# A vision tower on one core: weight splits at bursts 25 and 31 of an attention batch in place of 0 and 30, and a second buffer of raw weights in the sequence experts

## The chip, the core and the metric

The kernel runs on one core of a Trainium2 chip. The core has five engines that run side by side, each with its own list of instructions in order: TensorE (PE, matmuls and transposes), VectorE (DVE), ScalarE (ACT), GpSimd (POOL) and SyncE (SP). SP and POOL also issue DMA transfers. The engines meet at semaphores: an instruction can wait until a counter has reached a number, and everything behind it on its engine waits with it. The metric is the device time of one execution in microseconds (us); lower is better.

## The reference, cut to what matters

Two layers over x of 8 images with 1024 tokens each, 128 wide, in float32. Each layer is an attention and a mixture of 8 experts of which 2 are used (per image in the first layer, per token in the second).

```python
h = _L0_tok_ref(x, L0_tok_W)                       # embedding + position table
h = h + _L0_attn_ref(_layernorm(h), Wq, ..., gamma, beta)   # 8 heads, 1024 x 1024 scores per head pair
h = h + _L0_ffn_ref(_layernorm(h), ..., w1, b1, w2, b2)     # 2 of 8 experts per image
h = h + _L1_attn_ref(_layernorm(h), ...)                    # block attention
h = h + _L1_ffn_ref(_layernorm(h), Wr, W1, b1, W2, b2)      # 2 of 8 experts per token
```

The weights of all 16 experts (w1, w2 of the first layer, W1, W2 of the second: 32 matrices of 64 Ki floats) are used in matmuls as a sum of two parts, a high part rounded to the matmul's float32r format and a low part with the rest. The kernel makes these parts itself, one matrix (a "job") at a time, and stores them in HBM, from where the two expert stages load them.

## The kernel before

**Stages.** One after the other: a start (embedding of image 0), the first attention over 8 batches (one image each) with the embedding of the next image between its bursts, the sequence experts (first mixture), the block attention, the token experts (second mixture), and the sum of the results.

**Attention.** A batch is 32 bursts of two units. A unit is a pair of score matmuls on PE (L874) into PSUM, one exponential on ACT (L787) and four matmuls with the values (L886). PE, ACT and DVE each walk through the bursts in the same written order. The table STEPS (L549) puts the next image's work between them: "E" at bursts 1 and 3 (PE L802 embeds half an image into the PSUM bank psA; DVE L958 reads it, adds the position table and takes moments), "T" at 5 and 13 (PE L808 transposes), "q", "k", "N", and "v" at 27 and 29 (PE L823, read by DVE L976). All of these use the one bank psA: a step's matmuls wait until DVE has read the step before it (semaphore psA_free). At the start of each quarter (bursts 0, 8, 16, 24) DVE also adds a projected context (add_input, L460) and divides (L1069 to L1075); at the end of each quarter (7, 15, 23, 31) it takes the output out of PSUM (out_of_psum, L1065). At burst 28 POOL multiplies and adds tiles of the residual (L473 to L477).

**A weight job.** POOL loads a raw matrix into the tile raw (load_raw, L223), DVE splits it into the tile split (split_weights: a copy that rounds, L229, and a subtraction, L231), POOL stores split to HBM (store_split, L236) and at once issues the load of the next job, which may overwrite raw since the split is done. DVE's split waits until the job's raw matrix has landed (raw_in) and until the store of the job before has landed (split_out). There is one raw tile and one split tile. In attention the table SPLIT (L553) says at which bursts of a batch DVE and POOL do their part of a job: 2 jobs per batch, 16 in all, at the end of the burst's other work. Job 0 is loaded by POOL after it has cleared a tile for batch 1 (L760, L763).

**Sequence experts.** 32 items (image, half, expert); per item PE does 24 matmuls, ACT eight Gelu passes and an output (L1215), DVE four subtractions (L1295), each of which frees a tile that ACT writes again, and a weighted add (L1487). The class Rest places the other 16 jobs, one per item, at items 13 to 28, between the third and the fourth subtraction. SP loads the chosen experts' weights (1 MB each, L1434).

Of the kernel before, what the change touches and what calls it, by code (L numbers as in the profile page):

```python
# [8 lines left out]
F32 = mybir.dt.float32  # L9
F32R = mybir.dt.float32r  # L10
# [3 lines left out]
ALU = mybir.AluOpType  # L14
# [3 lines left out]
P = 128  # L18
EPS = 1e-5
CH = 512  # L20
# [5 lines left out]
class Tally:  # L26


    def __init__(self, start, parity=0):
        self.start, self.count, self.parity = start, 0, parity  # L30
# [128 lines left out]
class Shared:  # L159
# [8 lines left out]
    def __init__(self, nc, ctx, B, S, D, E):  # L168
        c = Core(nc, ctx, "ag")
        T, K = S // P, 2  # L170
        self.nc, self.B, self.T, self.K, self.E, self.D = nc, B, T, K, E, D
        self.JOBS = [(stage, e, layer) for stage in range(2) for e in range(E) for layer in range(2)]
        self.FIRST_JOBS = 2 * E
        self.raw, self.split = c.sb("raw", [P, CH]), c.sb("split", [P, 2, CH], F32R)
        self.raw_in, self.split_done = c.sem("raw_in"), c.sem("split_done")
        self.aw_sum = c.sb("aw_sum", [P, 1])
        self.n0 = [c.sb(f"n0{p}", [P, T, D]) for p in range(2)]
        self.res = [c.sb(f"res{p}", [P, TPC, D]) for p in range(2)]
        self.pe_tab = c.sb("pe_tab", [P, T, D])
        self.qs0, self.ks0 = (c.sb(n, [P, T, T // 2 * P], F32R) for n in ("qs0", "ks0"))  # L180
        self.w_in0 = [c.sem(f"w_in0{r}") for r in range(K)]
        self.f, self.f_done = self.n0[0][:, TPC:2 * TPC, :], c.sem("f_done")
        self.brow = c.sb("brow", [P, 5, D])
        self.w_raw = c.sb("w_raw", [D, 4, D])
        self.o_n, self.ctxT = c.sb("o_n", [P, CH]), c.sb("ctxT", [D, 2, P])
        self.stat_f, self.mv_f = c.sb("stat_f", [P, TPC, 6]), c.sb("mv_f", [P, TPC, 2])
        self.veps_f, self.rs_f = c.sb("veps_f", [P, TPC]), c.sb("rs_f", [P, TPC])
        self.dctx = [nc.dram_tensor(f"contexts{i}", [D, 2, P], F32).ap() for i in range(2)]
        self.norm_done, self.ctx_out, self.ctx_in, self.op_done, self.split_out, self.bias_in = (c.sem(n) for n in (
            "norm_done ctx_out ctx_in op_done split_out bias_in".split()))  # L190
        self.var_f, self.root_f, self.normal_done, self.stream_done = (c.sem(n) for n in "var_f root_f normal_done stream_done".split())

        self.attn_b, self.ones = c.sb("attn_b", [P, 1]), c.sb("ones", [P, P])
        self.gate_w, self.gate_b = c.sb("gate_w", [D, E]), c.sb("gate_b", [B, E])
        self.lower, self.places = c.sb("lower", [B, E, E]), c.sb("places", [B, 2, K, E])
        self.sc, self.e_sc = c.sb("sc", [P, B, T]), c.sb("e_sc", [P, B, T])
        self.zs, self.rz, self.corr = (c.sb(n, [P, B]) for n in ("zs", "rz", "corr"))
        self.mx, self.mxT, self.mx_row, self.mx_all = (c.sb(n, [P, 32]) for n in ("mx", "mxT", "mx_row", "mx_all"))
        self.mx4, self.mx1 = c.sb("mx4", [32, 4]), c.sb("mx1", [32, 1])
        self.base = c.sb("base", [P, 2 * T])  # L200
        self.pooledT = c.sb("pooledT", [D, B])
        self.lg, self.pr, self.rk = (c.sb(n, [B, 1, E]) for n in ("lg", "pr", "rk"))
        self.beats, self.ties = c.sb("beats", [B, 1, E, E]), c.sb("ties", [B, 1, E, E])
        self.nmx, self.sm, self.rsm = c.sb("nmx", [B, 1]), c.sb("sm", [B, 1]), c.sb("rsm", [B, 1])
        self.sel, self.val = c.sb("sel", [B, K, E]), c.sb("val", [B, K, E])
        self.g2, self.i2, self.i2i = c.sb("g2", [B, K]), c.sb("i2", [B, K]), c.sb("i2i", [B, K], I32)
        self.d_gate = nc.dram_tensor("d_gate", [B, K], F32).ap()
        self.d_chosen = nc.dram_tensor("d_chosen", [B, K], I32).ap()
        (self.tab_in, self.shift_done, self.exp_done, self.sum_done, self.gate_ps, self.pool_done,
         self.pooled_done, self.top_done, self.two_done, self.gate_out, self.gate_in) = (c.sem(n) for n in (  # L210
            "tab_in shift_done exp_done sum_done gate_ps pool_done "
            "pooled_done top_done two_done gate_out gate_in").split())

    def size(self, i):
        return self.GROUPS[i][1] - self.GROUPS[i][0]

    def load_raw(self, pool, j, ins):
        stage, e, layer = self.JOBS[j]
        src = ins[("w1", "W1")[stage]][e] if layer == 0 else ins[("w2", "W2")[stage]][e].rearrange("(n p) d -> p n d", p=P)
        dst = self.raw[:, :] if layer == 0 else self.raw[:, :].rearrange("p (n d) -> p n d", d=self.D)  # L220
        if j:
            pool.wait_ge(self.split_done, j)
        pool.dma_start(dst, src).then_inc(self.raw_in, 16)  # L223

    def split_weights(self, dve, j):
        dve.wait_ge(self.raw_in, (j + 1) * 16)
        if j:
            dve.wait_ge(self.split_out, j * 16)
        self.nc.vector.tensor_copy(self.split[:, 0, :], self.raw[:, :])  # L229
        dve.drain()  # L230
        self.nc.vector.tensor_tensor(self.split[:, 1, :], self.raw[:, :], self.split[:, 0, :].bitcast(F32), ALU.subtract).then_inc(self.split_done, 1)  # L231

    def store_split(self, pool, j, experts):
        stage, e, layer = self.JOBS[j]
# [285 lines left out]
def embed_and_attend(nc, H, ident, half, mean1, rstd1, score1, experts, shared, gate, chosen, ins, B, S, D, NH):  # L520
# [29 lines left out]
             20: ("N", 0), 21: ("N", 1), 27: ("v", 0), 29: ("v", 1)}  # L550
    FIRST = [("E", 0), ("E", 1), ("T", 0), ("q", 0), ("k", 0), ("T", 1), ("q", 1), ("k", 1), ("N", 0), ("N", 1), ("v", 0), ("v", 1)]
    LATE = 2
    SPLIT = [{0: 0, 30: 1}] * (B - 1) + [{5: 0, 12: 1}]  # L553
    GATES = {1: "biased", 3: "shift", 7: "sums", 9: "weights", 22: "pooled", 24: "ranks", 25: "choice", 30: "rows"}
    POOLED = {10: (0, 0), 11: (0, 1), 13: (0, 2), 14: (0, 3), 17: (1, 0), 18: (1, 1), 19: (1, 2), 20: (1, 3)}
    PE_TILES = {17: (4, 0), 18: (4, 1), 19: (5, 0), 20: (5, 1)}
    E, HID = ins["w1"].shape[0], ins["w1"].shape[2]
    assert shared.FIRST_JOBS == sum(map(len, SPLIT)) and HID == CH
    RESCUE = 25
# [7 lines left out]
    with ExitStack() as ctx:  # L567
        c = Core(nc, ctx, "a0")
# [152 lines left out]
        def _(pool):  # L721
# [20 lines left out]
            def batch(b, par, prior, more):  # L742
                for m in range(BURSTS):
# [8 lines left out]
                    if more and m == RESCUE - 1:  # L752
                        send_guard(pool, b + 1, 1 - par)
                    if m in SPLIT[b]:
                        j = b * len(SPLIT[b]) + SPLIT[b][m]
                        shared.store_split(pool, j, experts)
# [186 lines left out]
        def _(dve):  # L943
# [155 lines left out]
            def batch(b, par, prior, more):  # L1099
                for m in range(BURSTS):  # L1100
# [23 lines left out]
                    if more and m == RESCUE - 1:  # L1124
                        guard(b + 1)
                    if m in SPLIT[b]:
                        shared.split_weights(dve, b * len(SPLIT[b]) + SPLIT[b][m])

# [278 lines left out]
def sequence_experts(nc, H, ident, half, mean1, rstd1, score1, gate, chosen, shared, experts, ins, B, S, D):  # L1407

    parts = experts[0]
    E, _, WIDE = parts.shape  # L1410
    NB = (WIDE - 1) // (4 * P)
    T = S // P
# [5 lines left out]
    with ExitStack() as ctx:  # L1418
        c = Core(nc, ctx, "f0")
        f, f_done = shared.f, shared.f_done  # L1420
        w = [[shared.first_slot(r, WIDE) for r in range(K)], [c.sb(f"w1{r}", [P, WIDE]) for r in range(K)]]
        x_ps, t_ps, t_read, y_done, freed = (c.sem(n) for n in "x_ps t_ps t_read y_done freed".split())
        w_in = [shared.w_in0, [c.sem(f"w_in1{r}") for r in range(K)]]
# [3 lines left out]
        @block.sync  # L1427
        def _(sp):
            def load_parts(b):
                for r in range(K):  # L1430
                    e = sp.value_load(chosen[0:1, b * K + r:b * K + r + 1], min_val=0, max_val=E - 1)
                    if b >= 2:
                        sp.wait_ge(y_done, (b - 2) * PER + (PER - K + r + 1))
                    sp.dma_start(w[b % 2][r][:, :], parts[bass.ds(e, 1), :, :].rearrange("o p c -> p (o c)")).then_inc(w_in[b % 2][r], 16)  # L1434

            shared.load_sums(sp, B * T // 2 - 1)
            for b in range(1, 5):
                load_parts(b)
            shared.spread_gates(sp, 1, gate, chosen)
            load_parts(5)  # L1440
            sp.wait_ge(shared.gate_in, 64)
            for b in range(6, B):
                load_parts(b)

        @block.gpsimd
        def _(pool):
            b = B - 1
            shared.root_finish(pool, b, 0, 1, half)
            shared.root_finish(pool, b, 1, 0, half)
            shared.root_finish(pool, b, 1, 1, half)  # L1450
            shared.token_power(pool, 1)
            shared.gate_power(pool, 1)
            for j in range(shared.FIRST_JOBS, len(shared.JOBS)):
                shared.store_split(pool, j, experts)
                if j + 1 < len(shared.JOBS):
                    shared.load_raw(pool, j + 1, ins)
            pool.wait_ge(shared.split_out, 4 * E * 16)
            pool.wait_ge(shared.bias_in, 32)

# [752 lines left out]
```

## Time and profile before

| what | value |
|---|---|
| time, median of 3 runs | 1415.1 us (1413.77 to 1416.4) |
| the profiled execution: its own time | 1412.59 us |
| the profiled execution: span of its instructions | 1410.8 us |
| PE busy | 1184.4 us, 84% |
| ACT busy | 992.8 us, 70% |
| DVE busy | 917.3 us, 65% |
| POOL busy | 556.0 us, 39% |
| mean granted clock of TensorE | 0.916 of full speed |

Busy shares are means over stages with different limits. A wait in the views is idle time of an engine just before an instruction, with what ended it; it costs time only where the engine, or whoever waits for it, is the bound of its stage. Times in the views are us from the start of the span, so the profiled execution's own time is 1.8 us longer than what they cover.

### The profile page before, as it was taken

How to read it: one execution, taken by the hardware profiler on the slowest of the kernel's cores; microseconds unless marked ns; L12 is line 12 of the kernel's file. 1: busy time of each engine (PE TensorE's matmuls, PEld its weight loads, DVE VectorE, ACT ScalarE, POOL GpSimd, SP SyncE). 2: the span in 40 equal slices, each digit the busy share in tenths (PEclk: the TensorE clock that was granted, in tenths of full speed). 3: DMA queues.
4: the chain of work that ended last, by engine and by line, in shares of the span. 5: the costliest groups of instructions: out<-in, count | busy, mean ns of one | idle time of the engine just before them, and what ended most of it. 6: DMA issues, size and time to landing. Idle time of an engine off the chain costs nothing. (4 is left out here: it accounts for less than half of the span.)

```text
span 1410.8 us, 26930 instructions
## 1 busy us (share of the span) xinstructions
PE 1184.4 (84%) x9386; PEld 795.3 (56%) x9386; DVE 917.3 (65%) x2573; ACT 992.8 (70%) x1348; POOL 556.0 (39%) x538
## 2 busy tenths in 40 slices
PE   3499999999999999979898966888861799999940
PEld 2245444444444444558777755777761688888830
DVE  4255767777877776678687766888641466666625
ACT  0389889898989899869787855444410799999930
POOL 3413333333233332121011111478776177777660
PEclk9899999999999999989999987798955899999975
DMA  3645554554637282132226510011116377777609
GB/s 87 118 110 127 117 129 107 127 131 102 152 80 169 64 170 64 39 128 92 88 85 232 178 50 1 18 41 47 45 48 237 119 238 240 234 251 238 239 25 357
DMA packets 93162, 180.56 MB, mean 128 GB/s; under 512 B 15597, under 2 KB 64200, under 8 KB 84960
## 3 DMA queue, kind: packets, MB, share of 16 engines
q1 hardware_dynamic: 72832, 129.18, 33.1%
q0 software_dynamic: 17344, 42.68, 9.1%
q10 hardware_dynamic: 2848, 6.95, 1.7%
q8 instruction: 76, 1.25, 0.4%
q14 instruction: 62, 0.51, 0.1%
HBM read 116.96 MB, written 63.12 MB: 128 GB/s over the span
## 5 line engine op out<-in xcount | busy, mean ns | idle before, releaser
L787 ACT ACTIVATE a_probs<-a_psS 128x1024 f32<-128x1024 f32 x512 | 482.4, 1035 | 69.0 <-PE a_psS L874 57.5
L886 PE MATMUL a_psO<-a_probs,a_v 128*32 128x256 f32 x4096 | 277.4, 388 | 1.1 <-issue 0.7
L1295 DVE TENSOR_TENSOR f_g_lo<-f_g,f_g_hi 128x512 fp32r<-128x512 f32 x284 | 193.5, 688 | 117.7 <-ACT f_g L1202 116.5
L2039 POOL DMA_INDIRECT result<-f_out,f_idx x156 | 181.2, 1162 | 98.4 <-issue 58.5
L886 PEld LDWEIGHTS a_psO<-a_probs,a_v 128*32 128x32 f32 x4096 | 107.5, 109 | 133.9 <-issue 85.4
L1595 POOL DMA_INDIRECT queue<-all_row,all_idx x128 | 125.2, 978 | 38.0 <-issue 37.4
L1199 ACT ACTIVATE f_g_hi<-f_psH,all_w 128x512 fp32r<-128x512 f32 x156 | 109.3, 701 | 19.8 <-PE f_psH L72 18.6
L1202 ACT ACTIVATE f_g<-f_psH,all_w 128x512 f32<-128x512 f32 x156 | 109.2, 700 | 0.0
L874 PE MATMUL a_psS<-ag_qs,ag_ks 50*128 50x512 f32 x512 | 96.7, 454 | 9.6 <-DMA ag_qs<-a_gparts 7.1
L874 PE MATMUL a_psS<-a_qs,a_ks 50*128 50x512 f32 x512 | 95.1, 447 | 4.0 <-ACT a_probs L787 1.5
L465 POOL TENSOR_TENSOR ag_rs_f<-ag_veps_f,all_half 128x4 f32<-128x4 f32 x32 | 33.3, 1042 | 133.6 <-DVE ag_veps_f L135 133.6
L874 PEld LDWEIGHTS a_psS<-ag_qs,ag_ks 50*128 50x128 f32 x512 | 39.7, 190 | 57.0 <-ACT a_probs L787 30.3
L236 POOL DMA_DIRECT2D experts<-ag_split x32 | 18.2, 568 | 132.4 <-DVE ag_split L231 132.4
L1209 ACT ACTIVATE f_x_hi<-f_psX 128x512 fp32r<-128x512 f32 x55 | 33.1, 601 | 52.6 <-PE f_psX L1234 43.6
L70 PE MATMUL f_psH<-f_x_hi,all_w 128*128 128x512 f32 x156 | 68.6, 440 | 0.0
L874 PEld LDWEIGHTS a_psS<-a_qs,a_ks 50*128 50x128 f32 x512 | 38.8, 186 | 50.5 <-ACT a_probs L787 36.7
L71 PE MATMUL f_psH<-f_x_lo,all_w 128*128 128x512 f32 x156 | 62.2, 399 | 0.0
L72 PE MATMUL f_psH<-f_x_hi,all_w 128*128 128x512 f32 x156 | 62.0, 398 | 0.0
L70 PE MATMUL f_psY<-f_g_hi,all_w 128*128 128x512 f32 x156 | 61.6, 395 | 0.0
L72 PE MATMUL f_psY<-f_g_hi,all_w 128*128 128x512 f32 x156 | 61.4, 394 | 0.0
L71 PE MATMUL f_psY<-f_g_lo,all_w 128*128 128x512 f32 x156 | 61.4, 393 | 0.0
L1199 ACT ACTIVATE f_g_hi<-f_psH,f_w 128x512 fp32r<-128x512 f32 x64 | 44.6, 697 | 19.2 <-PE f_psH L72 18.7
(370 smaller groups left out, 2619.7 us busy)
## 6 DMA issues: line engine op xcount, KB each, us to landing
all_w<-experts SPq DMA_DIRECT2D x39, 1026.5 KB, 5.4
experts<-ag_split POOLq DMA_DIRECT2D x32, 512.0 KB, 4.2
f_rows<-queue SPq DMA_DIRECT2D x39, 260.0 KB
f_w<-experts SPq DMA_DIRECT2D x8, 1026.5 KB, 5.9
qparts<-a_parts SPq DMA_DIRECT2D x16, 512.0 KB, 3.6
kparts<-a_parts SPq DMA_DIRECT2D x14, 512.0 KB, 3.1
ag_qs<-experts SPq DMA_DIRECT2D x4, 1026.5 KB, 5.2
ag_ks<-experts SPq DMA_DIRECT2D x4, 1026.5 KB, 5.0
```

Source lines behind the costliest of these rows:

```text
L70: nc.tensor.matmul(out, w_lo, x_hi, start=first, stop=False)
L71: nc.tensor.matmul(out, w_hi, x_lo, start=False, stop=False)
L72: return nc.tensor.matmul(out, w_hi, x_hi, start=False, stop=last)
L465: self.nc.gpsimd.tensor_tensor(self.rs_f[:, :], self.veps_f[:, :], half[:, 0:TPC], ALU.pow).then_inc(self.root_f, 1)
L787: nc.scalar.activation(probs[u % NPR][:, :], psS[score_buffer(u)][:, :, :].rearrange("p a n -> p (a n)"), ACT.Exp).then_inc(exp_done, 1)
L874: last = nc.tensor.matmul(psS[score_buffer(u)][:, p, :], ks[par][64 * p:64 * p + KG, kt, hp * P:(hp + 1) * P], queries(par, hp, p, a), sta ...
L886: last = nc.tensor.matmul(psO[32 * g:32 * g + 32, a * HALF:(a + 1) * HALF], v[par][:, 2 * hp + p, kt, :], probs[u % NPR][:, cols:cols + HA ...
L1199: nc.scalar.activation(g_hi[i][:, n, :], psH[n][:, :], ACT.Gelu, bias=bias(m, n))
L1202: nc.scalar.activation(g[:, n, :], psH[n][:, :], ACT.Gelu, bias=bias(m, n)).then_inc(g_done, 1)
L1295: nc.vector.tensor_tensor(g_lo[i][:, n, :], g[:, n, :], g_hi[i][:, n, :].bitcast(F32), ALU.subtract).then_inc(lo_done, 1)
L1595: pool.indirect_dma_start(queue, bass.IndirectOffsetOnAxis(ap=idx[n % NROW][:, k, t:t + 1], axis=0), row[n % NROW][:, k, t, :], None).then ...
L2039: pool.indirect_dma_start(result, bass.IndirectOffsetOnAxis(ap=idx[i][:, j:j + 1], axis=0), out[i][:, j, :], None, bounds_check=2 * B * S ...
```

## The change

In batches 0 to 6 the two jobs move from bursts 0 and 30 to bursts 25 and 31; in batch 7 they stay. In the sequence experts a second raw tile (raw1) is added: its jobs use the two tiles in turn, job 17 is loaded by POOL at the start of the stage, and after the store of job j POOL loads job j + 2 in place of j + 1. There is still one split tile. Each raw tile has a semaphore of its own.

```diff
-        self.raw, self.split = c.sb("raw", [P, CH]), c.sb("split", [P, 2, CH], F32R)
-        self.raw_in, self.split_done = c.sem("raw_in"), c.sem("split_done")
+        self.raw, self.split = [c.sb("raw0", [P, CH])], c.sb("split", [P, 2, CH], F32R)
+        self.raw_in, self.split_done = [c.sem(f"raw_in{p}") for p in range(2)], c.sem("split_done")
...
+    def raw_place(self, j):
+
+        if j < self.FIRST_JOBS:
+            return 0, j + 1
+        r, i = divmod(j - self.FIRST_JOBS, 2)
+        return i, r + 1 + (0 if i else self.FIRST_JOBS)
+
+    def raw_freed(self, j):
+
+        return j if j <= self.FIRST_JOBS else j - 1
+
     def load_raw(self, pool, j, ins):
...
         if j:
-            pool.wait_ge(self.split_done, j)
-        pool.dma_start(dst, src).then_inc(self.raw_in, 16)
+            pool.wait_ge(self.split_done, self.raw_freed(j))
+        pool.dma_start(dst, src).then_inc(self.raw_in[i], 16)
 
     def split_weights(self, dve, j):
-        dve.wait_ge(self.raw_in, (j + 1) * 16)
+        i, loads = self.raw_place(j)
+        raw = self.raw[i]
+        dve.wait_ge(self.raw_in[i], loads * 16)
         if j:
             dve.wait_ge(self.split_out, j * 16)
...
-    SPLIT = [{0: 0, 30: 1}] * (B - 1) + [{5: 0, 12: 1}]
+    SPLIT = [{25: 0, 31: 1}] * (B - 1) + [{5: 0, 12: 1}]
...
+        shared.raw.append(c.sb("raw1", [P, CH]))
...
         @block.gpsimd
         def _(pool):
+            shared.load_raw(pool, shared.FIRST_JOBS + 1, ins)
...
             for j in range(shared.FIRST_JOBS, len(shared.JOBS)):
                 shared.store_split(pool, j, experts)
-                if j + 1 < len(shared.JOBS):
-                    shared.load_raw(pool, j + 1, ins)
+                if j + 2 < len(shared.JOBS):
+                    shared.load_raw(pool, j + 2, ins)
```

The order on DVE from burst 29 of a batch to burst 1 of the next, in the kernel before (a_v is the value tile, ag_split the split tile, a_o_t and ag_o_n the output of a quarter, all_H the residual):

```order
L976 TENSOR_TENSOR a_v<-a_psA,ag_brow 128x32x16
L229 CAST ag_split<-ag_raw 128x512
L231 TENSOR_TENSOR ag_split<-ag_raw,ag_split 128x512
L1065 STREAM_TRANSPOSE a_o_t<-a_psO 128x512
L460 TENSOR_TENSOR ag_res<-a_psA,ag_n 128x256
L1069 RECIPROCAL a_rden<-a_o_t 128x16
L1071 TENSOR_TENSOR a_o_t<-a_o_t,a_rden 128x16x16
L1075 STREAM_TRANSPOSE ag_o_n<-a_o_t 128x512
L229 CAST ag_split<-ag_raw 128x512
L231 TENSOR_TENSOR ag_split<-ag_raw,ag_split 128x512
L958 TENSOR_TENSOR all_H<-a_psA,ag_pe_tab 128x512
```

The same place on DVE in the changed kernel, whose lines stand 15 further down (L244 and L246 are the split, L1080 is out_of_psum, L973 is E's read):

```order
L991 TENSOR_TENSOR a_v<-a_psA,ag_brow 128x32x16
L1080 STREAM_TRANSPOSE a_o_t<-a_psO 128x512
L244 CAST ag_split<-ag_raw 128x512
L246 TENSOR_TENSOR ag_split<-ag_raw,ag_split 128x512
L475 TENSOR_TENSOR ag_res<-a_psA,ag_n 128x256
L1084 RECIPROCAL a_rden<-a_o_t 128x16
L1086 TENSOR_TENSOR a_o_t<-a_o_t,a_rden 128x16x16
L1090 STREAM_TRANSPOSE ag_o_n<-a_o_t 128x512
L973 TENSOR_TENSOR all_H<-a_psA,ag_pe_tab 128x512
```

No split stands between the division and E's read any more; one split has moved from ahead of out_of_psum to behind it.

DVE at bursts 25 to 29 of a batch in the changed kernel (L528 to L532 end burst 25's other work, L513 begins add_bias of burst 26, L991 is v's read):

```order
L532 SCALAR_TENSOR_TENSOR all_score<-all_score,ag_rs_f 128x4
L244 CAST ag_split<-ag_raw 128x512
L246 TENSOR_TENSOR ag_split<-ag_raw,ag_split 128x512
L513 TENSOR_TENSOR ag_res<-ag_res,ag_brow 128x512
L130 BN_STATS ag_stat_f<-ag_res 128x6 x4
L133 BN_AGGR ag_mv_f<-ag_stat_f 128x2 x4
L135 TENSOR_SCALAR ag_veps_f<-ag_mv_f 128x4
L991 TENSOR_TENSOR a_v<-a_psA,ag_brow 128x32x16
```

The two rows of the split are new here; the others are those of before, in their old order.

POOL at the start of the sequence experts in the changed kernel (L480 a root, L286 and L292 the gates' powers, L251 the store, L236 the load; f_raw is the second raw tile):

```order
L236 DMA f_raw<-W 128x4x128
L480 TENSOR_TENSOR ag_rs_f<-ag_veps_f,all_half 128x4 x3
L286 TENSOR_TENSOR ag_e_sc<-ag_base,ag_sc 128x16
L292 TENSOR_TENSOR ag_pr<-ag_base,ag_lg 2x8
L251 DMA experts<-ag_split 128x1024
L236 DMA ag_raw<-W 128x512
L251 DMA experts<-ag_split 128x1024
L236 DMA f_raw<-W 128x4x128
```

The first row is new. The load that stands behind a store is now that of the job after the next, into the tile that the split just done has read.

## Rows read from the trace of the kernel before

**Rows 1.** Windows: stretch, length, busy us of each engine (instructions), PEclk, DMA share, GB/s.
```profile
55.00:600.00 545.00, 527.06 (x5657) 254.33 (x5658) 377.63 (x1075) 481.69 (x514) 172.19 (x179) 0.99 0.48 110
600.00:845.00 245.00, 214.01 (x1010) 169.56 (x1003) 182.17 (x423) 184.18 (x306) 34.58 (x44) 0.95 0.36 123
```

**Rows 2.** Waits of the whole span: total us, times, longest us.
```profile
ACT a_probs L787 <- PE a_psS L874: 57.5, 74, 6.7
...
PE a_psA L808 <- DVE all_H L958: 5.5, 6, 1.5
...
DVE ag_split L229 <- DMA ag_raw<-w: 31.9, 7, 21.5
...
DVE ag_split L229 <- DMA ag_raw<-W: 20.6, 12, 3.4
```

**Rows 3.** Timeline, bursts 1 to 5 of batch 0: start, us, what [idle before].
```profile
62.04 1.15 PE L802 MATMUL a_psA<-a_w_tok,a_xt 29*128 29x128 f32 x8
...
69.31 0.43 DVE L229 CAST ag_split<-ag_raw 128x512 fp32r<-128x512 f32 x1 [21.45 <-DMA ag_raw<-w]
...
70.59 0.69 DVE L958 TENSOR_TENSOR all_H<-a_psA,ag_pe_tab 128x512 f32<-128x512 f32 x1
70.79 0.57 POOL L236 DMA_DIRECT2D experts<-ag_split  x1 [5.46 <-DVE ag_split L231]
...
71.33 2.07 PE L802 MATMUL a_psA<-a_w_tok,a_xt 29*128 29x128 f32 x8 [4.81 <-DVE all_H L958]
...
78.58 0.66 PE L808 MATMUL a_psA<-all_ident,ag_n 128*128 128x128 f32 x4
```

**Rows 4.** Timeline, bursts 1 to 5 of batch 1.
```profile
135.30 1.15 PE L802 MATMUL a_psA<-a_w_tok,a_xt 29*128 29x128 f32 x8
...
138.51 0.69 DVE L958 TENSOR_TENSOR all_H<-a_psA,ag_pe_tab 128x512 f32<-128x512 f32 x1
...
145.69 0.66 PE L808 MATMUL a_psA<-all_ident,ag_n 128*128 128x128 f32 x4 [1.50 <-DVE all_H L958]
```

**Rows 5.** Timeline, burst 27 of batch 2 to burst 1 of batch 3.
```profile
259.75 0.69 DVE L976 TENSOR_TENSOR a_v<-a_psA,ag_brow 128x512 f32<-128x512 f32 x1
...
262.48 1.16 PE L823 MATMUL a_psA<-ag_w_raw,a_nT 128*128 128x128 f32 x8
...
265.41 1.62 DVE L231 TENSOR_TENSOR ag_split<-ag_raw,ag_split 128x512 fp32r<-128x512 f32 x1
...
267.02 0.72 DVE L1065 STREAM_TRANSPOSE a_o_t<-a_psO 128x512 f32<-128x512 f32 x1
...
268.43 0.42 DVE L460 TENSOR_TENSOR ag_res<-a_psA,ag_n 128x256 f32<-128x256 f32 x1 [0.69 <-PE a_psA L454]
...
269.78 0.71 DVE L1075 STREAM_TRANSPOSE ag_o_n<-a_o_t 128x512 f32<-128x512 f32 x1
...
270.99 1.15 PE L802 MATMUL a_psA<-a_w_tok,a_xt 29*128 29x128 f32 x8
```

**Rows 6.** The raw tile over the whole span: its loads, issue to landing.
```profile
DMA to landing us min/median/max: 3.9/4.5/8.4
```

**Rows 7.** Timeline, sequence experts: ACT's outputs of items 16, 26 and 28.
```profile
734.44 0.69 ACT L1215 ACTIVATE f_y<-f_psY,ag_qs 128x512 f32<-128x512 f32 x1
...
804.17 0.69 ACT L1215 ACTIVATE f_y<-f_psY,ag_qs 128x512 f32<-128x512 f32 x1
...
816.63 0.69 ACT L1215 ACTIVATE f_y<-f_psY,f_w 128x512 f32<-128x512 f32 x1
```

**Rows 8.** The split tile, the one store issued in 736:739 (at 737.2).
```profile
DMA to landing us min/median/max: 4.1/4.1/4.1
```

**Rows 9.** The split tile, the one store issued in 779:780 (at 779.1).
```profile
DMA to landing us min/median/max: 7.0/7.0/7.0
```

**Rows 10.** Timeline of SP, 736:785: its loads of expert weights, first issue and issue time.
```profile
738.12 2.11 SPq L1434 DMA_DIRECT2D f_w<-experts  x2
...
777.32 6.57 SPq L1434 DMA_DIRECT2D f_w<-experts  x2
```

More of the change, by code:

```diff
@@ L219, in load_raw @@
         src = ins[("w1", "W1")[stage]][e] if layer == 0 else ins[("w2", "W2")[stage]][e].rearrange("(n p) d -> p n d", p=P)
-        dst = self.raw[:, :] if layer == 0 else self.raw[:, :].rearrange("p (n d) -> p n d", d=self.D)
+        i, _ = self.raw_place(j)
+        raw = self.raw[i]
+        dst = raw[:, :] if layer == 0 else raw[:, :].rearrange("p (n d) -> p n d", d=self.D)
         if j:
-            pool.wait_ge(self.split_done, j)
-        pool.dma_start(dst, src).then_inc(self.raw_in, 16)
+            pool.wait_ge(self.split_done, self.raw_freed(j))
+        pool.dma_start(dst, src).then_inc(self.raw_in[i], 16)
     def split_weights(self, dve, j):
-        dve.wait_ge(self.raw_in, (j + 1) * 16)
+        i, loads = self.raw_place(j)
+        raw = self.raw[i]
+        dve.wait_ge(self.raw_in[i], loads * 16)
         if j:
             dve.wait_ge(self.split_out, j * 16)
-        self.nc.vector.tensor_copy(self.split[:, 0, :], self.raw[:, :])
+        self.nc.vector.tensor_copy(self.split[:, 0, :], raw[:, :])
         dve.drain()
-        self.nc.vector.tensor_tensor(self.split[:, 1, :], self.raw[:, :], self.split[:, 0, :].bitcast(F32), ALU.subtract).then_inc(self.split_done, 1)
+        self.nc.vector.tensor_tensor(self.split[:, 1, :], raw[:, :], self.split[:, 0, :].bitcast(F32), ALU.subtract).then_inc(self.split_done, 1)
     def store_split(self, pool, j, experts):
```

## The prediction

> **What bounds the kernel now.** I read the windows first, stage by stage. In the attention (55 to 600) PE is busy 527 of 545 us and ACT 482, in the sequence experts (600 to 845) PE 214 of 245, ACT and DVE some 183 each [rows 1]; no engine is full there, so each waits for another in turn, and a wait of PE for DVE is paid in time unless something later takes it up. Then the waits. In attention PE waits for DVE in one place that repeats: the transposes of step T for DVE's read of step E, 6 times, 5.5 us; ACT's longest wait for scores is 6.7 us [rows 2]. DVE itself waits for raw weights, 31.9 us in 7 splits of attention (21.5 of them at once) and 20.6 us in 12 splits of the sequence experts [rows 2]. The question is how much of these 52.5 us PE and ACT feel. The timeline of batch 0 answers for the largest: PE has E's matmuls done at 62.04 + 1.15 = 63.19, but DVE stands in the split of job 0 until its load lands at 69.31, and reads E at 70.59. PE needs the bank back for the second E, waits 4.81 us and goes on at 71.33 [rows 3]. That is the ACT wait of 6.7 us, since PE then offers no scores.
>
> **Batch 0, the first split moves to burst 25.** From the first E to T PE took 62.04 to 78.58 = 16.54 us [rows 3]. The same stretch of the program in batch 1 took 135.30 to 145.69, of which 1.50 is a wait treated below: 8.89 us [rows 4]. The difference is 7.65 us. It holds PE's wait and what came of it: the eight matmuls of E took 2.07 us behind the wait and 1.15 ahead of it [rows 3]. Without the split at burst 0 DVE can read E at 63.2, as soon as PE is done with it, and PE finds the bank free for the second E. The split then comes at burst 25, long after 69.31, when its raw matrix had landed even with this start [rows 3]. Saved: 7.65; I see nothing that takes more than 0.5 of it back.
>
> **Batches 1 to 6, the split at burst 0 is gone.** DVE reads E at 138.51 in batch 1, though PE had it ready at 135.30 + 1.15 = 136.45; DVE is 2.06 us late because of the wait for the load and the split itself. Two steps later PE waits 1.50 us at T for the same reason [rows 4]. DVE's work from E's read on is unchanged, so it comes 2.06 us earlier to the second E, more than the 1.50 that PE waited. All six waits together are 5.5 us [rows 2], and I take them as saved in full.
>
> What the moved splits cost: a split holds DVE for 70.59 - 69.31 = 1.28 us [rows 3]. At burst 31 it now stands between out_of_psum and add_input. Out_of_psum ends at 267.02 + 0.72 = 267.74, the split at 269.02, so add_input, which started at 268.43, comes 0.6 us later and ends at 269.44; PE's E at 270.99 needs it, 1.5 us of room. The division ended at 269.78 + 0.71 = 270.49 and now at 271.1, ahead of E's end at 270.99 + 1.15 = 272.14 [rows 5]. Nothing is paid. At burst 25 the split delays v's first read, which ended at 259.75 + 0.69 = 260.44; PE's second v needs the bank at 262.48, so 2.04 us of room against 1.28 [rows 5]. Nothing is paid here either, unless the split is stretched: beside POOL's arithmetic of burst 28 the subtraction took 1.62 us [rows 5] where an undisturbed split takes 1.28 in all. At burst 25 POOL issues DMAs instead, and what these do to a split no row shows; I take no stretch, and keep 1.62 against some 0.7 for the range.
>
> POOL's two issues per job, 0.57 us for a store [rows 3] and about as much for a load, move with the split, behind the guard rows of burst 24 and behind the residual of burst 28. POOL waits for DVE at these places, so they cost nothing.
>
> **Sequence experts, two raw tiles.** Items 16 to 28 took from 734.44 to 816.63, 82.19 us for 12 items; two of them near the end took 804.17 to 816.63 = 12.46 [rows 7], so 12 undisturbed ones would take 6 x 12.46 = 74.8. The excess is 7.4 us, against 20.6 us of DVE's waits [rows 2]: per wait 1.1 us is absorbed by DVE's slack in an item ((20.6 - 7.4) / 12), the rest is paid. With loads two jobs ahead this wait goes. The next in line is the split tile, of which there is still one: a split waits for the store of the job before. A store is issued 70.79 - 69.31 = 1.48 us after its split begins [rows 3]; with 4.1 us to land [rows 8] that is 5.6 us, within the 6.2 us of an item. With the slowest landing, 7.0 us [rows 9], it is 8.5, so 2.3 late, 1.2 after the slack. That store ran beside a pair of SP's loads of expert weights, and there are two such pairs in the stretch [rows 10]. So I expect 2 x 1.2 = 2.4 us left of the 7.4, and a saving of 5.0. The upper bound is all 7.4. For the lower: a load was issued only 0.57 us after its store [rows 3], so if the stores land as late as the loads did, 12 x 0.57 = 6.8 of the 20.6 go, which in the same proportion is 2.4 us of time.
>
> The Trainium skill (Trainium Kernel Development and Optimization, Best Practices) asks for double buffers so that DMA overlaps compute; read for the raw tile alone this gives the 7.4, and the rows of the store say that the other tile of the chain is still single.
>
> The load of job 17 at the head of the stage is one more issue on POOL, whose next work waits for DVE; no cost.
>
> **Sum.** 7.65 + 5.5 + 5.0 = 18.15 us. The profiled execution's own time was 1412.59 (span 1410.8 and 1.8 around it), so it would be 1394.4. It lay 2.5 us under the median of the runs, 1415.1; for the median I predict 1415.1 - 18.15 = 1397.
>
> **Rivals.**
> - The store takes the load's place in the sequence experts nearly in full: 2.4 saved there, 1399.6. For it: store and load were issued together and landed about as fast (4.1 and 4.5 at the middle) [rows 6, 8]. Against: at the middle landing the chain fits into an item.
> - The split at burst 25 makes PE late at its second v. Stretched to 1.28 + 0.7 + 0.9 = 2.9 us it exceeds the room of 2.04 by 0.9; in six batches 5.4 us, 1402.4. For it: the room is small and such stretches occur [rows 5]; against: not beside DMA issues, as far as rows show.
> - Slower: the second job's load, issued at burst 25, has not landed at burst 31. DVE then stands in the split with add_input and E's read queued behind it, and PE waits for the bank at E in each of 7 batches. The first split is done before 259.75, store and load are issued by about 261.1, the second split starts at 267.74 [rows 5]: 6.6 us to land, against 4.5 at the middle and 8.4 at most [rows 6]. With 1.5 us of room behind it, it costs something from a landing of 8.1 us; it undoes the 18.15 us, 2.6 a batch, at 10.7, and makes the kernel slower by over 0.2% (2.8 us, 0.4 a batch) at 11.1. At 12 us: 7 x 3.9 - 18.15, so 1424. The Trainium skill (SBUF — State Buffer, § SBUF: two separate sides, the warning "DVE blocks DMA") says that a DMA issued by POOL stalls while DVE copies float32 from SBUF to SBUF, since POOL cannot write its descriptors then, and gives some 620 ns alone against 3100 overlapped. With these 2.5 us on top of the longest landing, an estimate from the page, the load would take 10.9 us, PE would lose 2.8 us in each of 7 batches, and the time would be 1416.6; on top of the middle one it would cost nothing. No row shown here has a split beside such an issue.
> - No change: the waits go, but PE or ACT find as long a wait elsewhere, since the stages are chained by the gates and the stores of all 16 first jobs. What ends the attention (last burst, gates, last store) moves along with it, so I see no fixed point. 1415.
>
> **Chances.** The forecast 0.70, with a range of its own of 1392 to 1400: below it lies only the full 7.4 in the experts (1394.6) and the spread of the runs, above it 2 us of the moved splits. The store in the load's place 0.13; late at v 0.07; a gain beyond 1392 0.04; no change 0.03; slower 0.03. A measurement of this kernel can tell about 0.2% (2.8 us) from no change. The range to 1403 takes in the first two rivals, and 1391 below: it leaves out about 0.1. Faster 0.94, same 0.03, slower 0.03.
>
> **What would show it.** In the changed profile: no wait of DVE for a load of w; batch 0 with some 8.9 us from the first E to T, as in batch 1; no wait of PE at T for E's read, or under 1 us in all; v's second matmuls without a wait for DVE; in the sequence experts no wait for a load of W but some for the store, under 10 us together, with items 16 to 28 in 75 to 78 us. The prediction is wrong if PE waits for DVE at v or at E, if a split waits at burst 31, or if the waits for the stores come near the 20.6 us that went.

## The result, and the profile after

| kernel | median us | range, runs | ratio to before, 95% interval |
|---|---|---|---|
| before | 1415.09 | 1413.77 to 1416.4, 4 | |
| changed | 1400.92 | 1394.63 to 1402.1, 4 | 0.9889 [0.9862, 0.9916] |

The change is faster, by 14.2 us at the medians: inside the range to 1403, 3.9 us above the 1397 that was forecast. The profiled execution is the fastest of the four (1394.63, span 1392.8), 18.0 us shorter in span than the one profiled of before, so a part of its gain is not the change's. The balance by stages shows which.

Windows of the changed kernel, columns as in rows 1: from the first exponential to the end of batch 0, then batch 1, batch 6 and, to the end of its last exponential, batch 7.

```profile
53.60:120.20 66.60, 65.00 (x688) 30.80 (x686) 33.01 (x87) 60.31 (x64) 21.74 (x21) 0.96 0.54 112
120.20:186.30 66.10, 65.74 (x720) 31.83 (x712) 48.28 (x139) 60.21 (x65) 22.38 (x24) 1.00 0.54 124
450.70:516.90 66.20, 65.71 (x718) 31.84 (x712) 49.09 (x139) 60.18 (x65) 22.79 (x24) 1.00 0.51 122
516.90:585.25 68.35, 64.19 (x708) 30.96 (x700) 44.56 (x157) 60.49 (x67) 14.15 (x15) 0.98 0.17 52
```

The same view of the kernel before, batches 0, 1 and 7.

```profile
55.10:129.30 74.20, 67.80 (x688) 32.16 (x686) 33.74 (x88) 60.57 (x64) 22.66 (x22) 0.92 0.48 100
129.30:198.30 69.00, 66.49 (x720) 31.95 (x712) 49.81 (x140) 60.38 (x66) 23.46 (x25) 1.00 0.55 119
...
533.00:600.83 67.83, 64.21 (x708) 31.01 (x700) 45.24 (x156) 60.43 (x67) 13.21 (x15) 0.97 0.17 52
```

Batch 0 is 7.6 us shorter. Batches 1 to 6 took 533.0 - 129.3 = 403.7 and now 516.9 - 120.2 = 396.7, 7.0 less; PE is busy 65.74 of 66.10 us of batch 1, so it hardly waits there any more. The attention starts 1.5 us earlier and the part behind item 28 is 1.9 shorter, neither of which the change touches; batch 7 is 0.5 longer, and the stretch from its end to item 16, in which only the jobs of items 13 to 15 are touched, is 1.4 shorter. The sequence experts' items 16 to 28 took 82.19 [rows 7]; now, by ACT's outputs in the timeline:

```profile
717.51 0.69 ACT L1230 ACTIVATE f_y<-f_psY,ag_qs 128x512 f32<-128x512 f32 x1
...
730.30 0.69 ACT L1230 ACTIVATE f_y<-f_psY,ag_qs 128x512 f32<-128x512 f32 x1
739.12 0.69 ACT L1230 ACTIVATE f_y<-f_psY,ag_ks 128x512 f32<-128x512 f32 x1
...
764.56 0.69 ACT L1230 ACTIVATE f_y<-f_psY,f_w 128x512 f32<-128x512 f32 x1
774.22 0.69 ACT L1230 ACTIVATE f_y<-f_psY,ag_qs 128x512 f32<-128x512 f32 x1
781.60 0.69 ACT L1230 ACTIVATE f_y<-f_psY,ag_ks 128x512 f32<-128x512 f32 x1
...
800.49 0.69 ACT L1230 ACTIVATE f_y<-f_psY,f_w 128x512 f32<-128x512 f32 x1
```

800.49 - 717.51 = 82.98: nothing is saved. Two of the twelve items stand out, 8.82 and 9.66 us, where an undisturbed one takes 6.2; the one behind the second took 7.38. DVE's timeline shows why: its splits of the same stretch, with the idle time ahead of them in brackets.

```profile
724.71 0.43 DVE L244 CAST ag_split<-ag_raw 128x512 fp32r<-128x512 f32 x1 [0.64 <-DMA experts<-ag_split]
...
734.04 0.43 DVE L244 CAST ag_split<-f_raw 128x512 fp32r<-128x512 f32 x1 [4.47 <-DMA experts<-ag_split]
...
758.49 0.43 DVE L244 CAST ag_split<-f_raw 128x512 fp32r<-128x512 f32 x1 [0.85 <-DMA experts<-ag_split]
...
768.96 0.43 DVE L244 CAST ag_split<-ag_raw 128x512 fp32r<-128x512 f32 x1 [5.19 <-DMA experts<-ag_split]
```

The waits for a load are gone, and the waits for the store of the job before are there in their place. In the waits of the whole span (total, times, longest):

```profile
ACT a_probs L802 <- PE a_psS L889: 41.3, 66, 5.1
...
DVE ag_split L244 <- DMA experts<-ag_split: 14.6, 7, 5.2
```

They answer to ACT's 57.5 us and to the 31.9 and 20.6 us of DVE in rows 2; of these two there is no row any more. SP's timeline has the two pairs of expert loads between 721 and 760, beside which the two late stores were issued (726.2 and 759.97; the pairs landed 8.8 to 10.3 and 6.4 to 6.9 us behind their issues):

```profile
721.19 2.12 SPq L1450 DMA_DIRECT2D f_w<-experts  x2
...
759.37 6.39 SPq L1450 DMA_DIRECT2D f_w<-experts  x2
```

The view of the split tile gives their landings, in two windows that hold one store each:

```profile
DMA to landing us min/median/max: 7.7/7.7/7.7
...
DMA to landing us min/median/max: 8.9/8.9/8.9
```

### The profile page after: what moved, and what is told of

Read it like the earlier page. It is cut to its first block and busy times, and to the rows that moved or that the text cites. A ratio compares the mean times of both kernels' runs of the same rounds, so it can differ in the third digit from the quotient of the medians.

```text
span 1392.8 us, 26930 instructions
## 1 busy us (share of the span) xinstructions
PE 1176.3 (84%) x9386; PEld 790.6 (57%) x9386; DVE 908.9 (65%) x2573; ACT 992.5 (71%) x1348; POOL 556.1 (40%) x538
## 3 DMA queue, kind: packets, MB, share of 16 engines
q8 instruction: 76, 1.25, 0.4%
## 5 line engine op out<-in xcount | busy, mean ns | idle before, releaser
L480 POOL TENSOR_TENSOR ag_rs_f<-ag_veps_f,all_half 128x4 f32<-128x4 f32 x32 | 33.3, 1042 | 129.0 <-DVE ag_veps_f L135 128.9
L251 POOL DMA_DIRECT2D experts<-ag_split x32 | 18.3, 572 | 99.8 <-DVE ag_split L246 99.8
```

The lines of the kernel that those rows point to most:

```text
L480: self.nc.gpsimd.tensor_tensor(self.rs_f[:, :], self.veps_f[:, :], half[:, 0:TPC], ALU.pow).then_inc(self.root_f, 1)
```

## Experiments

Theory A: the table of bursts gives the whole gain; the second raw tile gives nothing, since the one split tile behind it holds the chain for as long, its stores landing late beside SP's loads. The rivals stand in the expectations.

**The table alone.** One raw tile, as before:

```diff
-    SPLIT = [{0: 0, 30: 1}] * (B - 1) + [{5: 0, 12: 1}]
+    SPLIT = [{25: 0, 31: 1}] * (B - 1) + [{5: 0, 12: 1}]
```

> The kernel before with the table of bursts alone changed (25 and 31), one raw tile. Theory A: all of the gain comes from here, 7.6 us in batch 0 and 5.5 to 7 in batches 1 to 6, so 13 to 15 us under the kernel before, and as fast as the changed kernel within 2 us. Rival B: the second raw tile gives the 5 us that the prediction gave it, and the table then only some 9 us.

Measured: 1399.34 (6 runs) beside 1414.93 for the kernel before, ratio 0.9884 [0.9841, 0.9927], as much as the whole change. Batch 1 to batch 5 take 66.1 us each, PE never waits at T for E's read, and the experts are as before (82.3 us for items 16 to 28):

```profile
DVE ag_split L229 <- DMA ag_raw<-W: 20.9, 12, 3.6
```

**The second raw tile alone.** The changed kernel with the old table:

```diff
-    SPLIT = [{25: 0, 31: 1}] * (B - 1) + [{5: 0, 12: 1}]
+    SPLIT = [{0: 0, 30: 1}] * (B - 1) + [{5: 0, 12: 1}]
```

> The changed kernel with the old table (bursts 0 and 30), two raw tiles in the sequence experts. Theory A: the wait for the store takes the place of the wait for the load, items 16 to 28 last 82 to 83 us as before, and the time is within 2 us of the kernel before. Rival B: 5 us under the kernel before, with items 16 to 28 in 75 to 78 us.

Measured: 1416.75 (12 runs), ratio 0.9993 [0.9964, 1.0022]: no difference. Items 16 to 28 took 84.1 us. The waits of its profile hold both kinds, that for w as before and that for the store as in the changed kernel:

```profile
DVE ag_split L244 <- DMA ag_raw<-w: 32.9, 7, 21.9
...
DVE ag_split L244 <- DMA experts<-ag_split: 15.0, 7, 5.6
```

**A second split tile in the sequence experts.** Jobs alternate between two split tiles there, so that a split waits for the store of the job before the last:

```diff
-        if j:
-            dve.wait_ge(self.split_out, j * 16)
-        self.nc.vector.tensor_copy(self.split[:, 0, :], raw[:, :])
...
+        if loads > 1:
+            dve.wait_ge(self.split_out[i], (loads - 1) * 16)
+        split = self.split[i]
+        self.nc.vector.tensor_copy(split[:, 0, :], raw[:, :])
...
+        shared.split.append(c.sb("split1", [P, 2, CH], F32R))
```

> The changed kernel with a second split tile in the sequence experts, used in turn like the raw tiles, so that a split waits for the store of the job before the last. Theory A: the waits for stores go, items 16 to 28 last 75 to 77 us, and the time is 6 to 8 us under the changed kernel, some 1393. Rival C: what slows these items is the traffic itself (SP's weight loads beside loads and stores), so the wait moves on to a load or to PE's expert weights, and the time is within 2 us of the changed kernel.

Measured: 1391.63 (6 runs), ratio 0.9837 [0.9797, 0.9877], the lowest median of the study. ACT's outputs of items 16 and 28 in its timeline are 75.10 us apart:

```profile
720.87 0.69 ACT L1232 ACTIVATE f_y<-f_psY,ag_qs 128x512 f32<-128x512 f32 x1
...
795.97 0.69 ACT L1232 ACTIVATE f_y<-f_psY,f_w 128x512 f32<-128x512 f32 x1
```

The only wait of a split left there is 0.24 us. One of its stores, issued at 728.84, still took 9.9 us to land; nobody waited for it. So the wait was the price, not the traffic as such. Two split tiles with one raw tile were not tried, so what the second raw tile adds beside them is not shown.

**The same splits on other items.** One split tile, as in the changed kernel, but no split in the two items behind the pairs of loads:

```diff
-    SPLITS = tuple(range(13, 29))
+    SPLITS = tuple(m for m in range(13, 31) if m not in (18, 23))
```

> The changed kernel, one split tile, with the jobs of the sequence experts at items 13 to 17, 19 to 22 and 24 to 30: no split, and so no store, at items 18 and 23, where in the changed kernel the two stores stood that took 7.8 and 8.9 us to land beside SP's loads of expert weights. Theory A (the stores beside SP's loads are what is late): items 16 to 28 in 75 to 78 us, waits for stores under 5 us in all, 4 to 7 us under the changed kernel. Rival E (any store of the chain is late once the load's wait is gone): items 16 to 28 stay above 80 us and the time within 2 us of the changed kernel.

Measured: 1392.27 (6 runs) beside 1412.53, ratio 0.9856 [0.9819, 0.9893]; items 16 to 28 in 75.6 us.

```profile
DVE ag_split L244 <- DMA experts<-ag_split: 0.8, 2, 0.5
```

Two places carried nearly all of the excess: the stores elsewhere nearly fit into an item, as the prediction had it. The late stores are those of the splits of items 17 and 22, and they stayed where they were: the first, issued at 728.22, still took 7.6 us to land, but the next split came an item later, so nobody waited for it. That median and the one of two split tiles don't differ by more than the runs can tell.

**Less traffic beside the stores.** SP's expert loads of batches 5 to 7 bring only the second half of their columns.

```diff
+                    part = slice(WIDE // 2, WIDE) if b >= 5 else slice(0, WIDE)
```

> The changed kernel, with SP's loads of the chosen experts' weights for batches 5 to 7 cut to the second half of their columns; the first half is left out, so the sequence experts use stale weights there. Theory A (traffic): with half of SP's bytes the two late stores land in 5 to 6 us instead of 7.8 and 8.9, and items 16 to 28 take 76 to 79 us. Rival F (POOL's descriptors are held up by DVE's copies, whatever SP loads): the stores stay at 8 us, items at 83 us.

Measured: 1391.9 (4 runs), ratio 0.9845 [0.9796, 0.9893]; items 16 to 28 in 75.5 us. The two stores landed in 4.9 and 7.1 us, with waits of 1.33 and 2.85 us in place of 4.47 and 5.19. In time it is as theory A says; one store came down as far as expected, the other stayed at 7.1 beside the pair issued at 759.71, so half the traffic does not undo all of the delay. Where a store falls against the pair matters too: with the full loads, stores issued 0.33 and 0.34 us ahead of this pair, in the runs with skipped items and with two split tiles, took 5.9 and 6.2 us, less than the 7.1 of the one issued 0.19 ahead of the halved pair; the store of rows 8, issued 0.9 ahead of its pair [rows 10], took 4.1. How the delay arises in full stays open.

**Batch 0 alone.** The kernel before, with the first split moved in batch 0 and nowhere else:

```diff
-    SPLIT = [{0: 0, 30: 1}] * (B - 1) + [{5: 0, 12: 1}]
+    SPLIT = [{25: 0, 30: 1}] + [{0: 0, 30: 1}] * (B - 2) + [{5: 0, 12: 1}]
```

> The kernel before with job 0 alone moved, from burst 0 to burst 25 of batch 0; job 1 stays at burst 30, all other batches at 0 and 30. Theory A: 7.6 us under the kernel before, batches 1 to 6 as they were, with the 5.5 us of PE's waits at T. Rival D: half of batch 0's excess is of another origin (the slow start of the stage) and the gain is 4 to 5 us.

Measured: 1408.73 (12 runs) beside 1414.93, ratio 0.9947 [0.9922, 0.9973], 6.2 us at the medians, and 3.8 to 11.0 by the interval, which excludes neither 7.6 nor rival D's 4 to 5. PE still waits at T in batches 1 to 6 (1.96, 0.54, 0.91, 0.42, 0.69 and 0.93 us), and these batches take 403.6 us, as before. So the table's gain has its two parts, batch 0 and the rest; the size of the first is not settled by this run. In its profiled execution batch 0 took 71.1 us, 3.2 under the kernel before and 4.5 over the changed one, though PE no longer waited: from 54.6 to 62.7 the granted clock was 0.50, and 0.57 from there to 71.5, so that the stretch from the first E to T took 12.2 us where the changed kernel took 8.8.

**Burst 30 in place of 31.** The changed kernel with `{25: 0, 30: 1}`.

> The changed kernel with the second job of batches 0 to 6 back at burst 30, ahead of out_of_psum; the first stays at 25. Theory A: what counted was the place at burst 0; the split at 30, stretched to 2.7 us beside POOL's arithmetic, still ends before PE's quarter does, so batches 1 to 6 stay at 66.1 to 66.3 us and the time is within 2 us of the changed kernel. Rival G: the stretched split delays out_of_psum and PE's next quarter, 0.5 us and more a batch, 3 us or more in all.

Measured: 1400.68 (10 runs), ratio 0.9905 [0.9872, 0.9938], against 1400.92 for the changed kernel: where the second split stands makes no difference that these runs show, and their interval is too wide to exclude the 3 us of rival G. The trace does that: batches 2 to 6 take 66.1 to 66.3 us, as in the changed kernel, where rival G asked for 0.5 us more in each. What counts is that burst 0 has none. Batch 1 took 67.4 us here and 66.1 in the changed kernel, without a wait of PE at T.

**No room for the second load.** The changed kernel with the first split at burst 29 and the second at 31, so that the second job's load has two bursts to land in place of six:

```diff
-    SPLIT = [{25: 0, 31: 1}] * (B - 1) + [{5: 0, 12: 1}]
+    SPLIT = [{29: 0, 31: 1}] * (B - 1) + [{5: 0, 12: 1}]
```

> The changed kernel with the first job of batches 0 to 6 at burst 29 in place of 25, so that the second job's load is issued only about 4 us before burst 31 asks for it. The prediction's slower rival in small: DVE waits 2 to 4 us for the load at burst 31, of which 1.5 us are room, so PE waits for E's bank about 1 to 2 us in each batch and the time is 6 to 14 us above the changed kernel. Rival H: the room behind burst 31 is larger, batches stay at 66 to 67 us and the time is within 2 us.

Measured: 1443.67 (6 runs), ratio 1.023 [1.0189, 1.0271], 43 us above the changed kernel. Its waits:

```profile
DVE ag_split L244 <- DMA ag_raw<-w: 33.0, 7, 5.2
...
PE a_psA L817 <- DVE ag_res L475: 18.3, 6, 3.3
```

The timeline at one of these places, the end of batch 2:

```profile
270.63 0.43 DVE L244 CAST ag_split<-ag_raw 128x512 fp32r<-128x512 f32 x1 [4.56 <-DMA ag_raw<-w]
271.75 0.42 DVE L475 TENSOR_TENSOR ag_res<-a_psA,ag_n 128x256 f32<-128x256 f32 x1
272.22 2.07 PE L817 MATMUL a_psA<-a_w_tok,a_xt 29*128 29x128 f32 x8 [3.09 <-DVE ag_res L475]
```

The mechanism is the one that the prediction's slower rival named: the split waits 4.56 us, add_input stands behind it, and PE loses 4.56 less the 1.5 of room, 3.06 (measured 3.09). The size was missed by far: 18.3 us of PE's waits, and 43 us of time. Batches 1 to 5 took 70.5 to 72.0 us, 4.4 to 6.0 longer than in the changed kernel; batches 6 and 7 were 10.4 and 8.7 longer, and since batch 7 has no E to wait with, these two hold something else as well, which stays open. The windows ahead of the place and behind PE's wait show the rest:

```profile
252.00:271.00 19.00, 16.95 (x192) 8.31 (x184) 10.39 (x26) 16.48 (x18) 8.32 (x10) 1.00 0.40 88
271.40:278.20 6.80, 5.98 (x32) 3.37 (x32) 4.64 (x17) 2.18 (x3) 2.12 (x3) 0.50 0.45 138
```

The granted clock is 1.00 ahead of the wait and 0.50 for 6.8 us from its end on. PE's 5.98 us of work there would take about half of that at the full clock; 3.09 + 2.99 = 6.1 is my estimate of the loss in a batch that has both. Batch 2 has: its E, too, came behind a wait, and from this E to the next passed 272.22 - 200.22 = 72.00 us, against 258.35 - 192.29 = 66.06 in the changed kernel, 5.9 more.

```profile
200.22 2.07 PE L817 MATMUL a_psA<-a_w_tok,a_xt 29*128 29x128 f32 x8 [3.10 <-DVE ag_res L475]
```

And in the changed kernel:

```profile
192.29 1.16 PE L817 MATMUL a_psA<-a_w_tok,a_xt 29*128 29x128 f32 x8
```

## Why the prediction was right, and where it failed

**Bound and batch 0: right.** From the first E to T the changed kernel took 69.44 - 60.62 = 8.82 us, where 8.89 was expected, and DVE reads E as soon as PE is done. PE's timeline, with DVE's read between:

```profile
60.62 1.15 PE L817 MATMUL a_psA<-a_w_tok,a_xt 29*128 29x128 f32 x8
61.81 0.69 DVE L973 TENSOR_TENSOR all_H<-a_psA,ag_pe_tab 128x512 f32<-128x512 f32 x1 [14.18 <-PE a_psA L817]
65.03 1.15 PE L817 MATMUL a_psA<-a_w_tok,a_xt 29*128 29x128 f32 x8
69.44 0.66 PE L823 MATMUL a_psA<-all_ident,ag_n 128*128 128x128 f32 x4
```

The stretch gave 16.54 - 8.82 = 7.72 (7.65 predicted), the batch 7.6. Moved alone, the same split gave 6.2 at the medians, and the profiled execution of that run began batch 0 at a granted clock of 0.50.

**Batches 1 to 6: right, a little small.** PE has no wait at T for E's read; the 5.5 us are saved, and 1.5 more. With the table alone the six batches took the same 396.7 us, and with the second raw tile alone 403.0, so the 7.0 are the table's. Batch 1 gives 2.9 of the 7.0, 1.4 more than its wait of 1.50; the other five give 4.1, where their waits were 4.0. What the 1.4 us of batch 1 were stays open: in the run with bursts 25 and 30, which has no split at burst 0, batch 1 was 1.3 us longer too.

**The moved splits: right.** The end of batch 2 in the changed kernel's timeline:

```profile
244.90 0.48 DVE L244 CAST ag_split<-ag_raw 128x512 fp32r<-128x512 f32 x1
...
248.68 0.69 DVE L991 TENSOR_TENSOR a_v<-a_psA,ag_brow 128x512 f32<-128x512 f32 x1
249.83 1.16 PE L838 MATMUL a_psA<-ag_w_raw,a_nT 128*128 128x128 f32 x8
...
255.02 0.83 DVE L244 CAST ag_split<-ag_raw 128x512 fp32r<-128x512 f32 x1
256.54 0.42 DVE L475 TENSOR_TENSOR ag_res<-a_psA,ag_n 128x256 f32<-128x256 f32 x1
258.35 1.15 PE L817 MATMUL a_psA<-a_w_tok,a_xt 29*128 29x128 f32 x8
```

At v the read ends at 249.37, 0.46 us ahead of PE's second v (0.76 expected), and PE does not wait. At burst 31 add_input ends at 256.96, ahead of E at 258.35 by 1.4. Nothing is paid, but the room at v is small. The second rival, a stretched split of 2.9 us at burst 25, did not come in: copy and subtraction took 1.25 us there (its price, besides, counted six batches where this split stands ahead of v in seven). The split at burst 31 did not wait for its load either, so the slower rival did not come in; the first split at burst 29 shows that it was a real one, and that its price, one us of time for each us of PE's wait, was too low.

**The sequence experts: the step that failed.** "So I expect 2 x 1.2 = 2.4 us left of the 7.4, and a saving of 5.0": the saving was -0.8. Right were the next wait in line (the store), the two places (SP's pairs of loads), and that the typical store nearly fits (the other five waits were 0.6 to 1.5 us). Of the signs that the prediction named, two failed: the waits for stores are 14.6 us in all, not under 10, and items 16 to 28 take 83.0, not 75 to 78.

Wrong was, first, the size of the wait at these places, 2.3 us, where 4.47 and 5.19 were measured. I took 7.0 us for the slowest landing from the kernel before, and the stores took 7.7 and 8.9 there; by the prediction's sum that makes 3.0 and 4.2. The rest is that I gave a store the whole 6.2 us of an item, while DVE was ready for its next split 734.04 - 4.47 - 724.71 = 4.86 and 768.96 - 5.19 - 758.49 = 5.28 us behind the start of the one before. The slack was not the fault: those two items were 8.82 and 9.66 us long against 6.2, 2.6 and 3.4 us more, so 1.8 us of each wait were absorbed, where I had put 1.1.

Wrong was, second, to spread the 7.4 us evenly over twelve waits. The kernel before shows its own two items beside the pairs, where a load was late (waits of 3.26 and 3.38 us):

```profile
740.79 0.69 ACT L1215 ACTIVATE f_y<-f_psY,ag_ks 128x512 f32<-128x512 f32 x1
749.33 0.69 ACT L1215 ACTIVATE f_y<-f_psY,ag_qs 128x512 f32<-128x512 f32 x1
...
782.69 0.69 ACT L1215 ACTIVATE f_y<-f_psY,f_w 128x512 f32<-128x512 f32 x1
791.34 0.69 ACT L1215 ACTIVATE f_y<-f_psY,ag_qs 128x512 f32<-128x512 f32 x1
```

They took 8.54 and 8.65 us, so 4.8 of the 7.4 lay there, and these places got worse by 1.3 us in all. In the ten other items the waits went from 14.0 to 4.9 us, and gave back only 0.5 (65.0 and 64.5 us).

The first rival, that the store takes the load's place (chance 0.13, 1399.6), is what happened, and even its lower bound, 2.4 us saved, was not reached: it had the stores land as late as the loads did, which took 6.5 and 6.6 us beside the pairs. With a second split tile the stretch takes 75.1 us, so the upper bound of 7.4 was sound (82.19 - 75.10 = 7.1); it only needed both tiles.

**Sum.** 7.6 + 7.0 - 0.8 from the windows, off the median of 1415.1, makes 1401.3; 1400.92 was measured. The term that failed (5.0 and 0.8) and the excess of batches 1 to 6 (1.5) account for the forecast's distance. That they do so to 0.4 us is partly luck, since the interval of the ratio leaves 3.8 us either way. The measured time lies just outside the 1392 to 1400 that the forecast, with its chance of 0.70, had for itself; the range to 1403 held because it took in the rivals.

The Trainium skill (DMA: Bandwidth & Descriptors, § Issuing engines are not separate DMA queues) says that transfers issued by different engines run on the same 16 DMA engines and interleave. The late stores of POOL beside SP's loads agree with it, 7.7 and 8.9 us against 4.1 at the middle of all 32 stores, as do the shorter waits with half of those loads.

## What to carry to other kernels

When a wait in a chain of load, work and store is taken away, cost the next wait of that chain with the transfers that will then run beside it, not with landing times of the kernel before; a second tile for one end of the chain gave nothing here until the other end had one too. Look also where the excess of a stage lies, item by item, before it is shared out among its waits. What waits for a late DMA can be moved out of its way as well as buffered: moving the two splits behind the late stores to later items gave as much as a second tile. And the room of a load should be read as a number ahead of a move, since a wait of PE that returns in every batch can cost nearly twice its length.

## What the runs showed of the hardware that was not expected

With the first split at burst 29, a wait of PE of 3.09 to 3.10 us per batch went with 5.9 us of time, since the granted clock was 0.50, the 1.2 GHz level, for 6.8 us behind it, and E's eight matmuls took 2.07 in place of 1.15 us. The Trainium skill (TensorE: Matmul & The Clock Gate, § HAM oscillation — how this bites in real kernels) describes a kernel that waits for a DMA in every tile and starts each one at the lower clock; this trace agrees, with a stretch at 0.50 behind each of PE's six waits.

The length of a batch varies between executions, and the granted clock with it. Batch 7, whose program no kernel here changes, took 68.3 us in the changed kernel at a granted clock of 0.98, and 76.9 in the one with the second raw tile alone, at 0.84, with 23.9 us on end at 0.50, in which PE was busy throughout. Windows of that run, the batch, and the stretch in it:

```profile
530.66:607.57 76.91, 73.37 (x708) 35.56 (x700) 46.76 (x160) 61.08 (x67) 13.84 (x16) 0.84 0.15 46
572.70:596.60 23.90, 23.90 (x150) 12.81 (x148) 8.21 (x30) 11.57 (x13) 1.04 (x1) 0.50 0.02 6
```

Why some executions get such a stretch and others don't stays open; it is as large as the terms that the study compares, so one profiled execution alone does not settle such a term.
